# Window attention on one core: the routing's sums taken from the raw image, its choice made inside the qkv products

## The reference

```
xn = groupnorm(x)                        # A * x + B per channel and image
q, k, v = xn @ W_qkv + b_qkv             # in 7 x 7 windows of 8 x 8 pixels
q_win, k_win = mean of q, of k over each window            # 49 x 128 each
r_idx = top_k(q_win * SCALE @ k_win.T, 4)                  # 4 key windows for each of 49
attn = softmax((q * SCALE) @ gathered k) per head          # 8 heads, 64 queries x 256 keys
o = attn @ gathered v
lepe = depthwise 3x3 convolution of v + lepe_b
x = x + (o + lepe) @ W_o + b_o
```

## Time and profile before

| | us |
|---|---|
| median of 3 runs (lowest, highest) | 3834.01 (3832.49, 3836.28) |
| the profiled execution's own time | 3842.81 |
| its span, first to last instruction | 3841.1 |
| PE busy, DVE busy, ACT busy, POOL busy | 3509.6, 2425.3, 2142.1, 1751.5 |
| layer 0: first qkv block of image 0 to last qkv block of image 7 | 18.4 to 1526.3 |
| from one image to the next (start of the qkv blocks of images 2 and 3) | 448.58, 658.28 |

### The profile page before, as it was taken

One profiled execution on the slowest core, in us unless ns is written; L12 is line 12 of the kernel. 1 busy time (PEld: TensorE's weight loads), 2 busy tenths in 40 slices (PEclk: granted clock), 3 DMA queues, 4 the chain that ended last, 5 costly groups with the idle time before them and its releaser, 6 DMA issues. The chain is left out here.

```text
span 3841.1 us, 106844 instructions
## 1 busy us (share of the span) xinstructions
PE 3509.6 (91%) x30518; PEld 2926.3 (76%) x30518; DVE 2425.3 (63%) x6251; ACT 2142.1 (56%) x5921; POOL 1751.5 (46%) x2967
## 2 busy tenths in 40 slices
PE   6989888888989898969999999999999969979999
PEld 3555555555545555549999999999999969979998
DVE  4868687786868686873333333333333349988998
ACT  4868788787868787864443333333333324435554
POOL 2737465574737373750002333333334436646665
PEclk9999999999999999989999999999999989989999
DMA  6222321313232322211110000000001110000000
GB/s 213 66 90 76 91 75 60 100 47 113 56 103 63 96 71 89 79 65 44 49 49 23 0 0 0 0 0 0 0 0 61 60 31 1 1 14 34 34 34 34
DMA packets 202873, 194.34 MB, mean 51 GB/s; under 512 B 35744, under 2 KB 191136, under 8 KB 199456
## 3 DMA queue, kind: packets, MB, share of 16 engines
q1 hardware_dynamic: 171168, 177.15, 14.7%
q10 hardware_dynamic: 31360, 12.87, 1.2%
HBM read 123.30 MB, written 66.58 MB: 49 GB/s over the span
## 5 line engine op out<-in xcount | busy, mean ns | idle before, releaser
L196 PE MATMUL bank<-h,w_hh 128*128 128x128 f32 x8032 | 933.8, 275 | 0.0
L196 PEld LDWEIGHTS bank<-h,w_hh 128*128 128x128 f32 x8032 | 917.0, 192 | 0.0
L1574 ACT ACTIVATE Pr<-bank,nmx 128x256 f32<-128x256 f32 x1568 | 722.3, 473 | 189.1 <-DVE nmx L1673 185.1
L241 ACT ACTIVATE h<-bank,bg 128x128 f32<-128x128 f32 x1008 | 370.2, 367 | 818.3 <-PE bank L196 818.2
L1511 POOL TENSOR_TENSOR Pr<-Pr,rden 128x512 f32<-128x512 f32 (+1 forms) x784 | 661.3, 855 | 180.1 <-DVE rden L1733 133.7
L1673 DVE TENSOR_REDUCE nmx<-bank 128x1 f32<-128x256 f32 x1568 | 553.7, 414 | 98.5 <-PE bank L1836 94.6
L1501 POOL COPY kg<-kT 128x64 f32 x1568 | 305.5, 238 | 547.5 <-DMA row<-ix 309.2
L287 DVE SCALAR_TENSOR_TENSOR inp<-bank,b_in,tz 128x256 f32<-128x256 f32 x196 | 85.8, 479 | 697.7 <-ACT tz L224 697.7
L1836 PE MATMUL bank<-kg,qT 32*128 32x256 f32 x3136 | 411.9, 440 | 31.1 <-POOL kg L1501 22.3
L1583 ACT ACTIVATE PT<-bank 128x512 f32<-128x512 f32 x784 | 428.7, 610 | 18.5 <-PE bank L1849 18.5
L1849 PE MATMUL bank<-ident,Pr 128*128 128x128 f32 x3136 | 438.3, 284 | 0.0
(11 more groups left out here) (261 smaller groups left out, 6421.1 us busy)
## 6 DMA issues: line engine op xcount, KB each, us to landing
v_rows<-v_padded SPq DMA_DIRECT2D x168, 232.0 KB, 3.3
vg<-v_windows SPq DMA_DIRECT2D x1176, 32.0 KB, 2.1
first_gates<-gate_sums SPq DMA_DIRECT2D x28, 512.0 KB, 2.6
gate_sums<-first_gates SPq DMA_DIRECT2D x28, 512.0 KB, 3.5
v_padded<-vpad SPq DMA_DIRECT2D x56, 232.0 KB, 2.4
X<-in_x SPq DMA_DIRECT2D x8, 1568.0 KB, 15.0
vg<-v_windows ACTq DMA_DIRECT2D x392, 32.0 KB, 2.2
x_backup<-X SPq DMA_DIRECT2D x8, 1568.0 KB, 6.0
```

What stands on the lines that cost most here:

```text
L196: ins = pe.matmul(bank[m][:, tt * COLS:(tt + 1) * COLS], w_hh[:, k, m * 128:(m + 1) * 128], prev[:, k, :], start=False, stop=(k == NH - 1) ...
L241: act.activation(h[:, 2 * q + tt, m, :], bank[m][:, tt * COLS:(tt + 1) * COLS], ACT.Tanh, bias=bg[:, 0, m:m + 1]).then_inc(s_h, 1)
L1574: act.activation(Pr[:, par, j, :], bank[j][:, 0:KEYS], ACT.Exp, bias=nmx[:, par, j:j + 1], accum_out=den[:, par, j:j + 1])\
```

## The change

- DVE's window sums are taken from `X` in image order, ahead of the normalisation, two blocks at a time in blocks 0 to 2 and the last in block 3. In block 3 DVE applies the norm to all 49 sums at once (`xsum = A * xraw + 64 * B`). ACT no longer waits for the sums before it overwrites `xb`.
- PE multiplies the sums inside block 4, into free columns of the banks of k and v; DVE makes `qs` and `ks` between the evacuations of k and v of that block. PE makes the logits in block 5, ahead of the v product; DVE evacuates them and takes the largest ahead of its evacuation of v, and the positions behind it.
- SP issues `row<-ix` at the start of its block 6, ahead of that block's stores; it was behind them.
- On PE the first depthwise block follows the qkv blocks at once and no longer waits for block 6 to be evacuated; the first scores do. The second depthwise block moves from before the scores of window 0 to behind them. ACT's copy of it moves behind the exponentials of window 0.

```diff
+            SUMS_AT = {0: (0, 1), 1: (2, 3), 2: (4, 5), 3: (6,)}
+            SUMS_BLOCK, LOGITS_BLOCK = 4, 5
...
+                            if b == LOGITS_BLOCK + 1:
+                                sp.wait_ge(s_tk, n * 3 + 4)
+                                passed(sp)
+                                sp.wait_ge(s_kg, (n * P2) + 1)
+                                passed(sp)
+                                sp.wait_ge(s_Tc, (n * P2) * 2 + 1)
+                                passed(sp)
+                                sp.dma_start(row[0:1, :], ix[:, 0:TOPK]).then_inc(s_row, 16)
...
-                        sp.wait_ge(s_tk, n * 3 + 4)
-                        passed(sp)
-
-                        sp.wait_ge(s_kg, (n * P2) + 1)
-                        passed(sp)
-                        sp.wait_ge(s_Tc, (n * P2) * 2 + 1)
-                        passed(sp)
-                        sp.dma_start(row[0:1, :], ix[:, 0:TOPK]).then_inc(s_row, 16)
...
                             act.wait_ge(s_pV, n * NBLK + b + 1)
-                            if b >= 2:
-                                act.wait_ge(s_qs, n * NBLK + b - 1)
...
-                        for b in range(2):
+
+                        def first_lepe(b):
                             act.wait_ge(s_lp, n * NBLK + b + 2)
                             act.activation(by_row(lp[:, b, :]), bank[7 - b][:, 0:BLK], ACT.Copy).then_inc(s_le, 1)
+
+                        first_lepe(0)
...
                         exps(0, 0)
+                        first_lepe(1)
                         with act.Fori(0, (P2 - 1) // 6) as k:
...
-                            dve.wait_ge(s_xb, n * NBLK + b + 2)
-                            dve.tensor_reduce(xsum[:, b * NWIN:(b + 1) * NWIN], xb[:, par, :]
-                                              .rearrange("p (w k) -> p w k", k=W2), AXX, ALU.add).then_inc(s_qs, 1)
+                            for k in SUMS_AT.get(b, ()):
+                                dve.tensor_reduce(xraw[:, k * NWIN:(k + 1) * NWIN],
+                                                  xblk(n, k).rearrange("p (r w c) -> p w r c", r=ROWS, c=WIN),
+                                                  mybir.AxisListType.XY, ALU.add).then_inc(s_qs, 1)
+                            if b == SUMS_BLOCK - 1:
+                                dve.wait_ge(s_id, n * IN_DVE + IN_DVE)
+                                dve.tensor_scalar(B64[:], Bb[:, bass.ds(n, 1)], float(W2), None, ALU.mult).then_inc(s_xs, 1)
+                                dve.wait_ge(s_xs, n * 2 + 1)
+                                dve.wait_ge(s_qs, (n + 1) * NBLK)
+                                dve.tensor_scalar(xsum[:], xraw[:], A[:, bass.ds(n, 1)], B64[:, 0:1], ALU.mult, ALU.add)\
+                                    .then_inc(s_xs, 1)
                             dve.wait_ge(s_pk, n * NBLK + b + 1)
...
                             dve.wait_ge(s_pv, n * NBLK + b + 1)
+                            if b == SUMS_BLOCK:
+                                for i, sums in enumerate((qs, ks)):
+                                    dve.wait_ge(s_wp, n * 2 + 2)
+                                    dve.tensor_scalar(sums[:], bank[1 + i][:, BLK:BLK + P2], b64[:, i:i + 1], None, ALU.add)\
+                                        .then_inc(s_ws, 1)
+                            if b == LOGITS_BLOCK:
+                                dve.wait_ge(s_lg, n + 1)
+                                dve.tensor_scalar(lg[:], bank[6][0:P2, BLK:BLK + P2], QSCALE / (W2 * W2), None, ALU.mult)\
+                                    .then_inc(s_tk, 1)
+                                dve.wait_ge(s_tk, n * 3 + 2)
+                                passed(dve)
+                                dve.max(m8[:], lg[:]).then_inc(s_tk, 1)
                             dve.tensor_scalar(vpad[:, 1 + b * ROWS:1 + (b + 1) * ROWS, 1:1 + W],
                                               bank[4 * par + 2][:, 0:BLK].rearrange("p (r c) -> p r c", c=W),
                                               vec[:, 2:3], None, ALU.add).then_inc(s_v, 1)
-                        for i, sums in enumerate((qs, ks)):
-                            dve.wait_ge(s_wp, n * 2 + 2)
-                            dve.tensor_scalar(sums[:], bank[0][:, i * P2:(i + 1) * P2], b64[:, i:i + 1], None, ALU.add)\
-                                .then_inc(s_ws, 1)
-                        dve.wait_ge(s_lg, n + 1)
-                        dve.tensor_scalar(lg[:], bank[1][0:P2, 0:P2], QSCALE / (W2 * W2), None, ALU.mult).then_inc(s_tk, 1)
-                        dve.wait_ge(s_tk, n * 3 + 2)
-                        passed(dve)
-                        dve.max(m8[:], lg[:]).then_inc(s_tk, 1)
-                        dve.wait_ge(s_tk, n * 3 + 3)
-                        dve.wait_ge(s_row, n * 16 + 16)
-                        passed(dve)
-                        dve.max_index(ix[:], m8[:], lg[:]).then_inc(s_tk, 1)
-
+                            if b == LOGITS_BLOCK:
+                                dve.wait_ge(s_tk, n * 3 + 3)
+                                dve.wait_ge(s_row, n * 16 + 16)
+                                passed(dve)
+                                dve.max_index(ix[:], m8[:], lg[:]).then_inc(s_tk, 1)
...
                             pe.matmul(bq[:, 0:BLK], w_qkv[:, 0:C], xs, start=True, stop=True).then_inc(s_pq, 1)
+                            if b == SUMS_BLOCK:
+                                pe.wait_ge(s_xs, n * 2 + 2)
+                                pe.matmul(bk[:, BLK:BLK + P2], w_qkv[:, 0:C], xsum[:], start=True, stop=True).then_inc(s_wp, 1)
                             pe.matmul(bk[:, 0:BLK], w_qkv[:, C:2 * C], xs, start=True, stop=True).then_inc(s_pk, 1)
-
+                            if b == SUMS_BLOCK:
+                                pe.matmul(bv[:, BLK:BLK + P2], w_qkv[:, C:2 * C], xsum[:], start=True, stop=True)\
+                                    .then_inc(s_wp, 1)
+                            if b == LOGITS_BLOCK:
+                                pe.wait_ge(s_ws, n * 2 + 2)
+                                pe.matmul(bv[0:P2, BLK:BLK + P2], qs[:], ks[:], start=True, stop=True).then_inc(s_lg, 1)
...
-                        pe.wait_ge(s_qs, (n + 1) * NBLK)
-                        pe.wait_ge(s_q, n * NBLK + NBLK)
-                        for i in range(2):
-                            pe.matmul(bank[0][:, i * P2:(i + 1) * P2], w_qkv[:, i * C:(i + 1) * C], xsum[:],
-                                      start=True, stop=True).then_inc(s_wp, 1)
-                        pe.wait_ge(s_V, n * NBLK + NBLK + 1)
-                        pe.wait_ge(s_v, n * NBLK + NBLK)
+                        pe.wait_ge(s_V, n * NBLK + NBLK)
...
                         for dx in range(3):
                             lepe(0, dx, bank[7])
-                        pe.wait_ge(s_k, n * NBLK + NBLK)
-                        pe.wait_ge(s_ws, n * 2 + 2)
-                        pe.matmul(bank[1][0:P2, 0:P2], qs[:], ks[:], start=True, stop=True).then_inc(s_lg, 1)
-                        for dx in range(3):
-                            lepe(1, dx, bank[6])
-                        pe.wait_ge(s_tk, n * 3 + 2)
...
+                        pe.wait_ge(s_v, n * NBLK + NBLK)
+                        pe.wait_ge(s_V, n * NBLK + NBLK + 1)
                         scores(0, 0)
+                        pe.wait_ge(s_tk, n * 3 + 2)
+                        for dx in range(3):
+                            lepe(1, dx, bank[6])
                         scores(1, 1)
                         turn(0, 0)
 
```

More of the change, by code:

```diff
@@ L1251, in program @@
             s_vst = [sem("v_stored_even"), sem("v_stored_odd")]
-            s_qs, s_bq = sem("window_sums"), sem("query_bias_ready")
+            s_qs, s_bq = sem("raw_window_sums"), sem("query_bias_ready")
+            s_xs = sem("window_sums_scaled")
             s_wp, s_ws = sem("window_sums_product"), sem("window_sums_ready")
@@ L1277, in program @@
             b64 = sb("bias_sums", [C, 2])
+            xraw = sb("raw_sum", [C, P2])
             xsum = sb("window_sum", [C, P2])
+            B64 = sb("shift_sums", [C, 1])
             ident = sb("ident", [C, C])
```

## The result

The changed kernel ran in 3801.98 us (median of 4, 3793.93 to 3802.73) against 3833.25 us before (4 runs, 3828.75 to 3836.28): a ratio of 0.9915, 95% interval 0.990 to 0.993. A second series with the unedited changed kernel gave 3798.5 against 3841.4, 0.9893 (0.9877 to 0.991). So it is 31 to 43 us faster, by the series. The forecast was 3790, the range 3777 to 3809.

What follows compares the result with a forecast made beforehand. PE bounds the qkv blocks; a serial chain from sums through route DMA to key copies sets the following stretch. Shorter stretches 42 plus clock 2 make 44 us: 3834.0 − 44 = 3790, range 3777 to 3809.

Steps and rivals of the forecast that it cites:

- Products and logits in blocks 4 and 5: Small products moved into PE's busy qkv blocks: 0.94 us per image, all on the path, bounds 0.5 and 0.94.
- Sums from X: DVE's strided reductions in blocks 0 to 3: 0.62 us each, nothing on PE, about 0.6 us later v stores.
- Routes on SP: Route transfer ahead of block 6's stores on SP: image 2's scores at 480.0 instead of 485.52, 5.5 us earlier.
- the 3.0 to 3.6 that was to show it: Sign of being right: eight stretches from the qkv products' end to the scores shrink to 3.0 to 3.6 us.
- ACT is late next: Before the first exponentials, ACT's v store wait and fourth gather limit image 2's gain to 4.96 us; exponentials at 481.75.
- The depthwise block behind the scores: Second block on PE: costs nothing at full clock; at the lower clock about 4.1 us, second window 1.5 to 2 late.
- Images: Shorter stretches: 4.75 us for each of six images, 6.7 each for images 0 and 5, together 42.
- The clock: Slow-clock first windows: some 9 us saved if all slow windows went; 2 us booked.
- Rival 1: Clock stays at its upper level through the first windows: 9 us instead of 2, giving 3783; chance 0.2.
- From the sum to the median: The 44 us was taken off the profiled 3842.8, giving 3798.8, and off the median 3834.0, giving 3790.
- Rival 2: Route transfer queues behind block 5's stores and lands 3 us later: gain 23 in all, 3811; chance 0.12.
- Rivals 3 and 4: 3: slow strided reductions make DVE bound qkv blocks, 3861, chance 0.04; 4: v stores still hold ACT, 3830, chance 0.03.

Runs made afterwards that it cites:

- early routes and the gathers on SP together: Changed kernel with SP issuing all window 0 gathers, ACT's waits behind its first exponentials, and routes ahead of block 5's v token stores: 3783.18 us, ratio 0.9860.
- the routes early alone: Changed kernel with the route transfer ahead of block 5's two v token stores, ACT's gather left in place: 3800.87 us, ratio 0.9916.
- the two experiments on the sums: Kernel before with only the sums from the raw image: 3838.91 us, ratio 1.0003; changed kernel with each raw reduction done twice: 3809.09 us, ratio 0.9925.
- the repetition: The changed kernel timed again without edits against the kernel before: 3798.5 us, ratio 0.9893.

## Why the prediction was right, and where it was off

- **Products and logits in blocks 4 and 5**, 0.94 per image: in images 1 to 7 block 4 takes 3.93 us from first product to first product and block 5 3.90, where both had 3.48, so 0.87 in all. Taking the measured durations was nearly right; little of them overlaps with their neighbours. The blocks as a whole grew by 7.4 / 8 = 0.93, which agrees by luck: single images grew by 0.36 to 1.95, and against the second profile of before it is 1.57. The difference is the clock over block 0, and block 3 of image 0.
- **Sums from X**: 0.61 us each, no price on PE. Right, also alone, and with a wider margin than the 3.49 against 2.62 that I gave, as the reductions overlap. The 0.6 us that I gave to the stores was not seen in block 6, whose copy ended 0.76 after the products, held by no store (the earlier trace rows had 1.95 us of wait there). I had expected 1.16.
- **Routes on SP**: issue predicted at -0.7, measured -0.83; keys 2.11 against 2.06; scores 2.96 against 2.88. Right. Seven of the eight stretches came out at 2.87 to 2.96, just under the 3.0 to 3.6 that was to show it, and image 0's at 3.79.
- **ACT is late next**: predicted 4.71, measured 4.98. The wait was the right one, as two experiments show. Two sizes were off and in part cancelled: the last store landed at 3.50 instead of 3.81, but ACT's gather began 0.87 behind that landing, not 0.40. The 0.40 was an estimate from POOL's start. In the trace of before ACT passes its last wait at 483.85 and issues the gather at 484.40, 0.55 later, 0.31 of it a load of its addresses. In the changed kernel it passes the wait for the last store at 469.24 and issues at 470.09, 0.85 later: two more waits, already met, stand between, at 0.15 each.
- **The depthwise block behind the scores** costs nothing at full clock: window 1's exponentials follow window 0's by 3.03 us in both kernels. Right, and the price at the lower clock, named as about 4.1 us, was 4.16 in image 2 when the pause came back (3.9 to 4.7 in all).
- **Images.** Five ordinary ones (1 to 4 and 6) gained 4.97 us in their period on average (3.7 to 6.7) against 4.75 + 0.25 forecast, image 5 gained 6.5 against 6.7, and image 0 only 4.4: its blocks took 38.7 us instead of 36.8. I had priced image 0 by its turn alone. While the input of the whole batch is loaded, ACT waits up to 10.5 us there for one store of v (9.8 before), and block 3 of image 0 took 9.9 to 12.5 us in the profiles of all kernels here, so its length says little of the change. The 6.7 for images 0 and 5 rests on the first profile, whose slow depthwise blocks the second does not have.
- **The clock**: 2 us booked, 1.7 found in the first windows. That is no confirmation: the first windows of before took 202.2 and 201.0 us in its two profiles, those of after 200.5 and 198.1, so the gain lies anywhere from 0.5 to 4.1. The granted clock of the first windows of image 2 went from 0.65 to 0.88; in image 1 it was 1.00:

```profile
468.58:483.06 14.48, 13.78 (x119) 8.27 (x119) 9.23 (x31) 10.48 (x39) 9.44 (x27) 0.88 0.26 67
264.62:279.10 14.48, 13.04 (x127) 7.77 (x131) 10.25 (x34) 11.37 (x41) 10.51 (x28) 1.00 0.25 66
```

  One slow piece stays in six of the eight images, over window 1's transposes:

```profile
477.47 1.94 PE L1863 MATMUL bank<-ident,Pr 128*128 128x128 f32 x8
...
481.43 1.09 PE L1863 MATMUL bank<-ident,Pr 128*128 128x128 f32 x8
```

  Rival 1 is a lever that is left: with early routes and the gathers on SP together, seven images ran their first windows at full clock, and first windows sum to 196.7 us there. That is 4 to 6 us less than in the kernel before, of the 9 that the prediction gave for all slow windows.
- **From the sum to the median.** This is the step that missed most. The sum against the profiled execution was 44, measured 41.5. The median came out 12 us above the forecast, since I took 44 off a median that stood 8.8 below the profiled execution; the profiled execution of after stood 0.6 below its own median. The second profile of before, 8.4 us shorter, says where such an offset lies: mostly in the clock over block 0 and in the turns. Against it the forecast 44 stands beside 33.1 measured: the turn gave 45.4, where the sum had 49.5 (42 and the 7.5 of the products in the blocks), and the blocks took 12.5 instead of 7.5. So the closeness of 41.5 to 44 is in part luck: the trace that the sum was read from was a long one of its kernel, by 8.8 us against the median beside it.
- **Rivals.** Rival 1 came in part. Rival 2 did not come: in image 2 the routes landed as fast as before (2.89 from issue to the first copy, 2.85 before), and within 0.06 of it in images 1 to 7. Its mechanism shows in image 0: there POOL sees the routes 2.38 us after their issue instead of 2.11, and with the routes issued behind block 5's padded rows 3.04 (3.28 with the routes early alone), when the stores ahead landed 2.70 (2.96) after that issue. The Trainium skill, DMA: Bandwidth & Descriptors, section Queues, rings and completion order, has descriptors consumed in ring order on each DMA engine and a completion that lands only after that engine's earlier writes. The trace agrees in image 0, but the DMA engines were full there around the issue (DMA share 1.08 from 54 to 56 us, counted by the transfers that start there, against 0.78 from 463.5 to 465.5 in image 2), and no run separates the two. In image 2 the stores ahead had landed at 466.21, 1.33 after the issue, and so held nothing; in image 7 one landed 2.48 after it and the routes were seen at 2.09, and no row shows which DMA engines each of the two used. Rivals 3 and 4 fell with the two experiments on the sums and with the turn itself.

## What to carry to other kernels

A serial chain between two busy phases is shortened best by starting its small transfer inside the phase before; here the place of one 0.9 us issue on one queue carried most of the gain (31 of 43 us were lost when it alone went back, part of them because the depthwise block had been moved behind it). After each such step, look for the instruction that waits next, in its queue and not only in the releaser that a row names: moving ACT's gather within ACT's own order brought nothing, giving it to an engine with time brought 0.9 us per image. When an engine's slack is spent, its cost may appear in the DMA stores that it feeds, two phases later. And a sum read from one trace should be set against that execution, and checked against a second trace of the same kernel before it is taken off a median.

## What the hardware showed that I had not expected

- The time lost to a late start of PE is larger than the delay. With the transfer late, behind a wait of 3.90 us the next depthwise block took 4.16 instead of 2.46 us, and the exponentials of window 1 came 4.8 us after window 0's instead of 3.03. On average the scores started 3.5 us later than in the repetition and those of window 8 4.2 later. Reordering moved most of this loss and removed 5 us of the expected 15.
- Two profiled executions of the same kernel differ by 8.4 us of span (3841.1 and 3832.7), mostly in the stretches where the granted clock changes, while the 40 windows behind them agree within 0.2 us over eight images.
- DVE's reductions of 0.61 us follow each other every 0.53 us, so the sum of the durations overstates a run of them by 15%.
